# State-space heads: unit matrix by one copy, picks and first updates one step on, a batch's scaling and half of the fadings on other engines

## What is computed

```python
proj = hidden_states @ W_in * mup_vector
z, xBC, dt = jnp.split(proj, [D_SSM, D_SSM + CONV_DIM], axis=-1)
xBC = jax.nn.silu(conv)                 # conv: 4 taps over time
x, Bm, Cm = ...                         # x: 64 heads of 8; Bm, Cm: 128
dt = jax.nn.softplus(dt + dt_bias)
dA = jnp.exp(dt * -jnp.exp(A_log))
def step(state, inp):
    state = state * dA_t[..., None, None] + (dt_t[..., None] * x_t)[..., None] * B_t[:, :, None, None, :]
    y_t = jnp.einsum('bghps,bgs->bghp', state, C_t)
y = ys + D.reshape(G, Hg)[..., None] * x
g = y * jax.nn.silu(z)
g = g * jax.lax.rsqrt(jnp.mean(jnp.square(g), axis=-1, keepdims=True) + EPS) * norm_w
out = g @ W_out
```

## Time and profile before

| | us |
|---|---|
| median of 3 runs | 1452.22 |
| lowest, highest | 1450.88, 1454.97 |
| profiled execution | 1456.39 |
| its span, first to last instruction | 1454.5 |
| first scan of the heads stage (start) | 883.64 |
| last additions to X in the heads stage (start) | 1152.30 |
| granted TensorE clock, mean over the span | 0.910 |

### The profile page before, as it was taken

The page is one execution under the profiler, slowest core; times in us unless marked ns, Lnnn a source line. Parts: engine busy times, 40 slices in busy tenths (PEclk is TensorE's granted clock), DMA queues, the critical chain, the costliest instruction groups (busy, mean ns, idle before and its releaser), DMA issues. The chain is left out here.

```text
span 1454.5 us, 32135 instructions
## 1 busy us (share of the span) xinstructions
PE 1177.6 (81%) x12288; PEld 887.3 (61%) x12288; DVE 980.0 (67%) x2086; ACT 638.3 (44%) x1497; POOL 615.7 (42%) x538
## 2 busy tenths in 40 slices
PE   2789898998864699999627985998989648999992
PEld 1356566665653498988613552665756437998881
DVE  6489798897877455555486847677687574555555
ACT  4366676676653133333345662343333223333341
POOL 0245455545430233333130295688796313333221
PEclk9899999999985699999958997899999859999996
DMA  4655756657523698665130002000000049966625
GB/s 157 156 133 157 179 157 174 162 161 174 155 83 88 235 423 304 255 218 215 64 137 8 25 14 47 13 17 2 2 2 1 16 101 397 420 232 246 252 91 184
DMA packets 96010, 212.87 MB, mean 146 GB/s; under 512 B 28721, under 2 KB 66866, under 8 KB 89714
## 3 DMA queue, kind: packets, MB, share of 16 engines
q1 hardware_dynamic: 86258, 188.26, 40.0%
q0 software_dynamic: 7488, 20.46, 4.0%
q10 hardware_dynamic: 2112, 2.10, 0.4%
HBM read 154.94 MB, written 38.54 MB: 133 GB/s over the span
## 5 line engine op out<-in xcount | busy, mean ns | idle before, releaser
L1226 ACT ACTIVATE ffn_h<-ffn_bank,ffn_b 128x256 f32<-128x256 f32 (+1 forms) x384 | 144.1, 430 | 276.1 <-PE ffn_bank L118 263.4
L1403 DVE CAST ffn_hh<-ffn_h 128x512 f16<-128x512 f32 (+1 forms) x192 | 73.7, 384 | 180.4 <-ACT ffn_h L1226 172.1
L1038 POOL DMA_INDIRECT ffn_xs<-xn_rows,ffn_from_rows x78 | 77.9, 998 | 264.7 <-PE ffn_bank L1121 178.8
L116 PE MATMUL ffn_bank<-ffn_hh,ffn_W 128*128 128x256 f16 (+1 forms) x768 | 180.8, 254 | 6.1 <-DVE ffn_hl L1405 6.0
L117 PE MATMUL ffn_bank<-ffn_hl,ffn_W 128*128 128x256 f16 (+1 forms) x768 | 180.7, 253 | 0.0
L118 PE MATMUL ffn_bank<-ffn_hh,ffn_W 128*128 128x256 f16 (+1 forms) x768 | 180.6, 253 | 0.0
L644 ACT ACTIVATE att_prob<-att_bank,att_nmax 128x512 f32<-128x512 f32 (+3 forms) x256 | 127.1, 525 | 29.5 <-DVE att_nmax L726 28.2
L733 DVE TENSOR_TENSOR att_ptl<-att_bank,att_pth 128x384 f16<-128x384 f32 (+1 forms) x192 | 114.2, 595 | 34.4 <-ACT att_pth L651 34.4
L651 ACT ACTIVATE att_pth<-att_bank 128x384 f16<-128x384 f32 (+1 forms) x192 | 101.4, 528 | 80.2 <-PE att_bank L591 80.2
L2129 ACT ACTIVATE ssmh_windows<-ssml_dtx 64x64 f32<-64x64 f32 x256 | 64.8, 253 | 152.2 <-PE ssm_Y L2028 144.9
L1045 POOL DMA_INDIRECT y_rows<-ffn_y,ffn_to_rows x78 | 76.8, 985 | 129.1 <-DVE ffn_y L1414 99.2
(11 more groups left out here) (355 smaller groups left out, 3251.9 us busy)
## 6 DMA issues: line engine op xcount, KB each, us to landing
ffn_W<-split_w SPq DMA_DIRECT2D x46, 2048.0 KB
att_piece<-in_ffn_w SPq DMA_DIRECT2D x32, 512.0 KB, 5.2
split_w<-att_halves SPq DMA_DIRECT2D x32, 512.0 KB, 4.3
att_Q<-att_pair SPq DMA_DIRECT2D x64, 128.0 KB, 2.4
ffn_back<-y_rows SPq DMA_DIRECT2D x16, 512.0 KB, 6.1
att_KB<-att_krl SPq DMA_DIRECT2D x8, 512.0 KB, 5.5
att_Q<-att_pair SPq DMA_DIRECT2D x64, 64.0 KB, 2.1
xn_rows<-ffn_XN SPq DMA_DIRECT2D x8, 512.0 KB, 2.6
```

Source lines behind the costliest of these rows:

```text
L116: pe.matmul(out, ah, bh, start=start, stop=False)
L1226: ins_ = act.activation(h[layer][:, m, 0:n], bank[1 + 2 * layer + u][:, (m % 2) * n:(m % 2 + 1) * n], ACT.Gelu, bias=bias[:, ds(e + m, 1)])
```

## The change

Projection: POOL scales batches 0 and 1 only. Heads:

- ACT scales batches 2 and 3: batch 2 in steps 24, 26, 28 and 30, batch 3 in 40 to 46 as before. PE waits for it from block 8 on.
- `ident8` is made from `one_hot` by one copy of 128 partitions, not from the unit matrix by two of 64. `one_hot` has a 1 in column p mod 64.
- The picks of pairs 4 to 15 are made after the scan of step 1.
- Batch 0's updates go from steps 0 to 6 to steps 1 to 7, its first carry from 7 to 8 (the next stay at 10, 13, 15), blocks 0 and 1 are opened in steps 1 and 2.
- For batches 1 to 3 the fadings of odd chunks stay on POOL but go ahead of the step's `mult`; those of even chunks go to DVE, behind the state addition of the step. The waits of `take_update` follow.
- The fourth carry of batches 1 to 3 is at step 9 of the batch instead of 10, the output of batches 0 to 2 begins at 41 instead of 42; the additions to X stay in steps 45 and 47.

```diff
@@ -1879,8 +1879,8 @@
 
             for n in range(NT):
                 weigh(n)
-                if n in (TB, 2 * TB):
-                    scale_x(n // TB)
+                if n == TB:
+                    scale_x(1)
 
         @block.sync
         def _(sp):
@@ -1961,15 +1961,15 @@
             return q, at // 4 * 2 + at % 2, at // 2 % 2
 
 
-        updates = {c: (0, c) for c in range(NC - 1)}
-        inters = {at: (0, q) for q, at in enumerate((7, 10, 13, 15))}
+        updates = {c + 1: (0, c) for c in range(NC - 1)}
+        inters = {at: (0, q) for q, at in enumerate((8, 10, 13, 15))}
         for b in range(1, B):
             updates |= {PAIRS_B * (b - 1) + 16 + 2 * c: (b, c) for c in range(NC - 1)}
-            inters |= {PAIRS_B * b + at: (b, q) for q, at in enumerate((-2, 2, 6, 10))}
+            inters |= {PAIRS_B * b + at: (b, q) for q, at in enumerate((-2, 2, 6, 9))}
         finishes = {PAIRS_B * b + at: (b, q) for b in range(B)
                     for q, at in enumerate((13 if b == 0 else 11, 19, 27, 35 if b + 1 < B else 34))}
-        opens = {0: 0, 1: 1, 4: 2, 14: 3} | {PAIRS_Q * (n - 2) + 4: n for n in range(XB, B * XB)}
-        outputs = {PAIRS_B * b + (42 if b + 1 < B else 41): b for b in range(B)}
+        opens = {1: 0, 2: 1, 4: 2, 14: 3} | {PAIRS_Q * (n - 2) + 4: n for n in range(XB, B * XB)}
+        outputs = {PAIRS_B * b + 41: b for b in range(B)}
         LAST = NP + 16
         half = lambda x: slice(x * CH, (x + 1) * CH)
 
@@ -2062,8 +2062,8 @@
 
                 if n >= YB:
                     pe.wait_ge(gated, n - YB + 1)
-                if n >= (B - 1) * XB:
-                    pe.wait_ge(x_scaled, n - (B - 1) * XB + 1)
+                if n >= 2 * XB:
+                    pe.wait_ge(x_scaled, n - 2 * XB + 1)
                 pe.matmul(Y[:, n % YB, :, :].rearrange("p c n -> p (c n)"), identf[:, :], skip[:, n, :], start=True,
                           stop=False).then_inc(skip_added, 1)
 
@@ -2169,9 +2169,9 @@
                     ins.then_inc(select_made, 1)
                 if p in inters:
                     keep_decay(*inters[p])
-                if p in (40, 42, 44, 46):
-                    q = (p - 40) // 2
-                    x = skip[:, (B - 1) * XB + q, :]
+                if p in (24, 26, 28, 30, 40, 42, 44, 46):
+                    q = p % 8 // 2
+                    x = skip[:, (2 + (p >= 40)) * XB + q, :]
                     act.activation(x, x, ACT.Copy, scale=d_col[:, q:q + 1]).then_inc(x_scaled, 1)
                 if p - 1 in finishes:
                     square_up(*finishes[p - 1])
@@ -2183,14 +2183,10 @@
             dve.tensor_tensor(one_hot, identf[:, 0:SH], identf[:, SH:], ALU.add).then_inc(hot_made, 1)
             dve.wait_ge(hot_made, 1)
             dve.tensor_scalar(pick(0, 4), hot(0, 4), UNSCALE, None, ALU.mult).then_inc(picks_made, 1)
-            for par in range(2):
-                rows = slice(par * CH, (par + 1) * CH)
-                dve.tensor_copy(ident8[rows, :].rearrange("p (c n) -> p c n", n=CH),
-                                identf[rows, rows].unsqueeze(1).broadcast_to([CH, 2 * TB, CH])).then_inc(ident_made, 1)
-            dve.tensor_scalar(pick(4, SH // 4), hot(4, SH // 4), UNSCALE, None, ALU.mult).then_inc(picks_made, 1)
+            dve.tensor_copy(ident8[:, :].rearrange("p (c n) -> p c n", n=CH), one_hot.unsqueeze(1).broadcast_to([P, NC, CH])).then_inc(ident_made, 1)
             dve.memset(ones[:, :], 1.0).then_inc(ones_done, 1)
             dve.memset(ssum[:, :], 0.0).then_inc(sum_cleared, 1)
-            dve.wait_ge(ident_made, 2)
+            dve.wait_ge(ident_made, 1)
 
             def split_decays():
                 dve.wait_ge(ft_high, 1)
@@ -2224,7 +2220,10 @@
                         dve.wait_ge(inter_psum, b * XB)
                     dve.tensor_copy(by_halves(states[:, 0, :]), grown).then_inc(state_done, 1)
                 else:
-                    dve.wait_ge(pool_faded if b else faded, (b - 1 if b else 0) * (NC - 2) + c)
+                    if b and c % 2:
+                        dve.wait_ge(pool_faded, (b - 1) * (TB - 1) + (c + 1) // 2)
+                    else:
+                        dve.wait_ge(faded, c if b == 0 else NC - 2 + (b - 1) * (TB - 1) + c // 2)
                     dve.tensor_tensor(by_halves(states[:, c, :]), by_halves(states[:, c, :]), grown, ALU.add).then_inc(state_done, 1)
 
             def read_inter(b, q):
@@ -2266,6 +2265,8 @@
             for p in range(LAST):
                 if p < NP:
                     scan(p)
+                if p == 1:
+                    dve.tensor_scalar(pick(4, SH // 4), hot(4, SH // 4), UNSCALE, None, ALU.mult).then_inc(picks_made, 1)
                 if p == 3:
                     split_decays()
                 if p == 5:
@@ -2276,7 +2277,7 @@
                     take_update(*updates[p - 2])
                 if p - 1 in updates and updates[p - 1][0] == 0:
                     take_update(*updates[p - 1])
-                if p in updates and updates[p][0] == 0 and updates[p][1]:
+                if p in updates and updates[p][1] and (updates[p][0] == 0 or updates[p][1] % 2 == 0):
                     fade(*updates[p])
                 if p in finishes:
                     gate_block(*finishes[p])
@@ -2284,10 +2285,10 @@
                     read_squares(*finishes[p - 6])
                 if p - 1 in outputs:
                     invert_root(outputs[p - 1])
-                if p - 3 in outputs:
-                    add_output(outputs[p - 3], 0)
-                if p - 5 in outputs:
-                    add_output(outputs[p - 5], 1)
+                if p - 4 in outputs:
+                    add_output(outputs[p - 4], 0)
+                if p - 6 in outputs:
+                    add_output(outputs[p - 6], 1)
 
         @block.gpsimd
         def _(pool):
@@ -2314,10 +2315,10 @@
             weigh(0, 0)
             weigh(0, 1)
             for p in range(LAST):
+                if p in updates and updates[p][0] and updates[p][1] % 2:
+                    fade(*updates[p])
                 if p < NP:
                     mult(p)
-                if p in updates and updates[p][0] and updates[p][1]:
-                    fade(*updates[p])
                 if p + 2 in updates and updates[p + 2][1] % 2 == 0:
                     b, c = updates[p + 2]
                     if (b, c) != (0, 0) and (b, c) != (0, 2):
```

## The result

The changed kernel takes 1445.6 us (median of five runs, 1443.2 to 1447.0), the kernel before 1452.62 on the same chip (1450.88 to 1454.97). The ratio is 0.9946 with a 95% interval of 0.9928 to 0.9964: faster, by 7.0 us. Another set of twelve runs of it on another chip gave 0.9954 (0.9938 to 0.9969). The forecast was 1446.6.

A forecast was written before the change was run, and what follows sets the result against it. It took POOL to bound the end of projection, and PE and the DVE-POOL state updates to alternate in the heads batches. Gains of 1.4 + 1.25 + 3.0 = 5.65 us took the median 1452.22 to 1446.6 us, range 1440 to 1453.

The forecast's parts named there:

- Projection: End of projection: without four scalings POOL ends 1.4 us earlier, not 6.2, as ACT's copies are late next.
- Rival (c): Projection: another engine holds the border, so the 1.4 us are not had; 1448.0 us, chance 0.07.
- First scan: Start of heads: one copy and the later pick leave the path; the first scan starts 2.0 us earlier.
- Hand-over: Heads, steps 0 to 18: second read of a carried sum comes 1.25 us earlier, what stays of 2.8.
- rival (a): More gain: PE's upper clock in the hand-over and the tie won in the batches; 11.2 us at most, 1443.8, chance 0.20.
- Fadings: Heads, batches 1 to 3: even fadings on DVE end waits for POOL; 1.0 us a batch, 3.0 in all.
- the tie: Batch 2, at 1000.9: POOL's mult goes ahead of DVE's second fading; if DVE wins, 2.4 us gained.
- DVE fadings of 1.2 to 1.9 us: Sign of being right, batches 1 to 3: DVE's fadings take that long beside a busy POOL.
- from there PE is the bound, so its 0.96 us count: Batch 2, behind addition 6: PE's next carry follows at once, so the addition's 0.96 us earlier end is gained.
- Edits at nothing: Heads: carry at step 9, output from 41, earlier root, B row load, counts and semaphore change no time.
- Rival (b): Batches: fadings on DVE cost what the waits cost, 1.45 us each; 2.65 us left, 1449.6, chance 0.25.
- Rival (d): Slower: PE idles around steps 9 to 12, stays at 1.2 GHz to step 17; 4.4 us slower, 1456.6, chance 0.06.

The follow-up runs named there:

- u_scaling: Changed kernel with batch 2's scaling by D back on POOL in the projection stage: 1444.34 us, 0.9925 of the kernel before.
- u_ident: Changed kernel with the two half copies of the unit matrix and the second pick back ahead of the first scan: 1451.53 us, 0.9969 of the kernel before.
- before_again: The kernel before, unchanged, run again for a second profile: 1452.93 us, 0.9992 of the kernel before.
- d_all: Changed kernel with every fading of batches 1 to 3 on DVE, none on POOL: 1461.73 us, 1.0046 of the kernel before.
- after: The changed kernel itself, in its first profile: median 1445.6 us, 0.9946 of the kernel before.
- u_updates: Changed kernel with batch 0's updates, first carry and opened blocks one step back, as before: 1449.02 us, 0.9950 of the kernel before.
- d_behind: Changed kernel with the odd fadings on POOL behind mult, not ahead of it: 1445.55 us, 0.9932 of the kernel before.

## Why the prediction was right

The forecast of 1446.6 lies 1.0 us above the 1445.6 measured. Step by step:

- **Projection, 1.4 us: right.** 1.29 in the profile, 1.37 when undone (u_scaling). What comes late next is ACT's first copy, as said. Rival (c) is out.
- **First scan, 2.0 us: right.** 2.11, and 2.11 to the second read when undone (u_ident). The one copy took 1.28 us in a range of 0.3 to 2.5.
- **Hand-over, 1.25 us with the first scan in it: the steps right, the total not.** 3.93 in the profiles. With equally fast products it is 1.32 to 1.71 (before_again), with the loss at the first sum there (DVE's wait for ACT at 909.85); of that 2.11 are the start's, and the shift costs 0.79, as the prediction's 2.0 and 1.25 also have it. The other 2.6 us are a 9.5 us stretch at 1.2 GHz in the first profile of the kernel before. The prediction named this end and gave it to rival (a); the step that failed is "as the clock before". What one execution's clock did was taken as what the kernel does.
- **Fadings, 3 x 1.0 us: the mechanism right, two sizes off, in opposite directions.** All the waits for POOL went. Batch 1's stretch fell by 0.76 (0.7 said), with DVE fadings of 1.07 to 1.33 us. Batches 2 and 3 fell by 2.54 and 2.53: the tie, taken as lost, was won, for which the prediction had 2.4. There the sign "DVE fadings of 1.2 to 1.9 us" failed: they took 0.69 to 0.95, and POOL waited instead. But "from there PE is the bound, so its 0.96 us count" was too generous to the change: 0.6 to 0.7 us of each stretch were given back behind it. From copy to copy 0.16 and 1.81 were left, in batch 3 1.81 by the profiles without the stretch at 195 us (57.85 - 56.04) and 0.20 with it. That is 3.8 us at best and 2.2 in the profile shown, around the 3.0 forecast.
- **Edits at nothing: right.** The carry moved to step 9 is the fourth, not the third. ACT's scaling and PE's wait for it changed no distance; the output order moved 0.1 to 0.2 us either way.
- **Not in the sum:** the last 1.2 GHz stretch of the stage, 6.8 us instead of 3.9, cost 1.28 at the tail. At 1.2 GHz the squares took 1.83 us instead of 1.02 and the projection's first sixteen products 5.84 instead of 5.38.

The sum, 1.29 + 3.93 + 0.16 + 1.81 + 0.20 - 1.28 = 6.1 us, is near the 5.65 forecast. But the hand-over is 2.7 us more than its term, the fadings 0.8 less than theirs, and the tail is a loss of 1.3 that had no term; the first and the last come from PE's clock. To that extent the hit is luck. Rival (a) had both of its conditions (tie won in two batches of three, fast products), but not its 11.2 us, since part was given back behind the additions and at the tail. Rival (b), fadings that cost what the waits cost, came near in batch 1 (3.61 us against 4.4), and d_all shows it, and worse, when DVE has them all. Rival (d) had the right mechanism in the wrong place: 1.2 GHz stretches decide several us here, but in the batches, at the tail and in the kernel before at the first carry. In the changed kernel PE did run at 1.2 GHz for 10.2 us in the first steps, but ahead of the first carry, and not through the work up to step 17.

## What to carry to other kernels

When several engines are each near full in turn, read the change of a stretch and the change from one batch to the next apart: a stretch made 2.5 us shorter gave 1.8, and below 21.5 us nothing. Move half of a job to the neighbour engine, not all of it: three fadings kept DVE 2.3 us and made the stretch 2.5 shorter (in batch 1, where they met POOL's work, 3.6 us and 0.8 shorter), six kept it 8.7 us and made it 3.8 longer than before (27.15 against 23.34). Take two profiles of the baseline before a term of some us rests on it, and compare distances between marks inside the changed stage; a part undone can look like a gain in time when the clock of another place moved.

## What the runs showed of the hardware

**A stretch at 1.2 GHz is priced by its place.** The granted clock was 0.51 to 0.54 in such windows. Where it began 13 to 18 us behind a batch's first state copy, in the stretch of additions where DVE and POOL are the bound, 3.2 to 3.7 us of it cost nothing: copy to copy is 61.77 with one (u_scaling, at 67) and without (after). Where it began 21 us behind the copy, in PE's own part (after, at 195 - 173.9), 3.6 us cost 1.6. Stretches of 7 us that began 26 us behind it cost 3.0 to 3.2. Parts that do not touch PE moved these stretches, so undone parts do not sum to the whole: the changed kernel, u_scaling and u_updates have the same 22.44, 20.80 and 20.80 us and the same copy-to-copy distances, and stages of 270.15, 268.08 and 269.09 us, the last of them in spite of a hand-over 1.8 us longer. What sets off such a stretch, the runs don't tell.

**A tie of 0.02 us goes to the first.** DVE's fading at 989.49 took 0.69, POOL's mult at 989.51 took 1.79 instead of 1.27. The other way round, the fading takes 1.38 to 1.53 (the earlier trace rows and d_all). The prediction had given the tie to POOL because it was ready first; which one is first is settled by hundredths of a microsecond that a sum doesn't hold. It is no coin toss, though: with this placement of the fadings that fading took 0.69 us in batches 2 and 3 in all seven profiles. With the odd fadings behind mult (d_behind) it came 0.42 us after a mult's start, at 992.88 behind 992.46, and took 1.39.
